# A fused attention kernel: the first unit's maxima move in among the last projections

## The reference

```
q, k, v = x @ Wq.T, x @ Wk.T, x @ Wv.T          # 32 heads of 16
q, k    = rope(q), rope(k)
scores  = q k^T / 4 + bias[head, i - j]          # bias where 0 <= i - j < 256, causal
m       = max(max_j scores, offset[head])
p       = exp(scores - m);  out = (p v) / (sum p + exp(offset - m))
x1      = layernorm(x + out @ Wo.T)
result  = layernorm(x1 + mxfp4(x1) @ mxfp4(Wff).T + bff)
```

## Time and profile before

| | |
|---|---|
| median of 3 runs | 1731.51 us (1725.53 to 1735.53) |
| profiled execution | 1733.33 us |
| its span, first to last instruction | 1731.5 us |
| busy: PE, DVE, ACT, POOL | 86%, 74%, 51%, 15% |
| mean granted TensorE clock | 0.932 of full |

### The profile page before, as it was taken

One profiled execution on the slowest core, in us unless ns is written; L12 is line 12 of the kernel. 1 busy time (PEld: TensorE's weight loads), 2 busy tenths in 40 slices (PEclk: granted clock), 3 DMA queues, 4 the chain that ended last, 5 costly groups with the idle time before them and its releaser, 6 DMA issues.

```text
span 1731.5 us, 60636 instructions
## 1 busy us (share of the span) xinstructions
PE 1497.2 (86%) x22568; PEld 858.3 (50%) x22576; DVE 1286.1 (74%) x3807; ACT 877.9 (51%) x1168; POOL 263.2 (15%) x120
## 2 busy tenths in 40 slices
PE   5978887838999999899999899999899999888773
PEld 4766666612555445455455455455455454443331
DVE  4454545469888788788788788788788883489996
ACT  3333333310665566566566565566566667445442
POOL 4434343440000000000000000000000000044543
PEclk9988898855999999999999999999999999999995
DMA  5444444475363273154245245345344402012221
GB/s 187 144 146 145 146 142 150 127 183 76 76 102 54 60 111 62 53 106 75 52 90 88 56 79 78 67 76 84 72 75 74 83 25 94 25 49 97 73 73 48
DMA packets 127101, 155.94 MB, mean 90 GB/s; under 512 B 18240, under 2 KB 82880, under 8 KB 126560
## 3 DMA queue, kind: packets, MB, share of 16 engines
q1 hardware_dynamic: 126816, 152.12, 38.3%
HBM read 100.78 MB, written 50.50 MB: 87 GB/s over the span
## 4 chain that ended last, share of the span: by engine, by line
PE 44%; DVE 23%; issue 19%; POOL 7%; ACT 3%; DMA 1%; DVEq 1%; SPq 0%; ACTq 0%; POOLq 0%
PE ps L728 10%; PE ps L707 10%; PE ps L687 10%; PE ps L713 6%; DVE junk L1211 6%; DVE mx L1204 4%; POOL probs L1076 4%; PE ps L660 4%; PE ps L820 2%; POOL h_lo L1062 2%; PE ps L738 1%; DVE mx L1211 1%; DVE probs L1178 1%; DVE parts L1155 1%; POOL probs L1116 1%
## 5 line engine op out<-in xcount | busy, mean ns | idle before, releaser
L929 ACT ACTIVATE probs<-ps 128x1024 f32<-128x1024 f32 (+3 forms) x768 | 603.2, 812 | 383.2 <-PE ps L713 332.6
L1211 DVE CUSTOM_DVE_ANT_0 junk<-ps,bias_q 128x384 bf16<-128x384 f32 (+2 forms) x1024 | 500.0, 502 | 123.0 <-PE ps L687 104.2
L687 PE MATMUL ps<-stack 96*32 96x384 bf16 (+3 forms) x6144 | 524.7, 341 | 59.6 <-DVE mx L1211 32.4
L707 PE MATMUL ps<-stack 99*32 99x512 bf16 (+3 forms) x6144 | 519.4, 333 | 11.8 <-issue 9.4
L1204 DVE TENSOR_REDUCE mx<-ps 128x1 f32<-128x128 f32 (+3 forms) x768 | 362.5, 485 | 27.0 <-PE ps L687 22.0
L713 PE MATMUL ps<-toep,flip 96*32 96x384 bf16 (+2 forms) x5120 | 374.9, 284 | 1.9 <-issue 1.8
L728 PE MATMUL ps<-probs,v_sb 128*32 128x512 f32 (+3 forms) x3072 | 322.0, 490 | 0.1
L687 PEld LDWEIGHTS ps<-stack 96*32 96x32 bf16 x6144 | 171.8, 97 | 298.9 <-DVE mx L1211 105.0
L707 PEld LDWEIGHTS ps<-stack 99*32 99x32 bf16 x6144 | 170.8, 96 | 140.4 <-issue 70.9
L1111 POOL TENSOR_TENSOR stack<-stack,bias_q 128x1024 f32<-128x1024 f32 x16 | 37.6, 2347 | 1110.1 <-ACT stack L989 1110.1
L713 PEld LDWEIGHTS ps<-toep,flip 96*32 96x32 bf16 x5120 | 146.9, 99 | 58.8 <-issue 7.5
(11 more groups left out here) (97 smaller groups left out, 1440.9 us busy)
## 6 DMA issues: line engine op xcount, KB each, us to landing
stack<-q_parts SPq DMA_DIRECT2D x192, 128.0 KB, 4.2
stack<-k_parts SPq DMA_DIRECT2D x192, 128.0 KB, 4.2
v_dram<-v_sb SPq DMA_DIRECT2D x32, 512.0 KB, 2.7
v_sb<-v_dram SPq DMA_DIRECT2D x128, 128.0 KB, 4.0
q_parts<-parts SPq DMA_DIRECT2D x96, 128.0 KB, 1.9
k_parts<-parts SPq DMA_DIRECT2D x96, 128.0 KB, 2.0
h_raw<-hT SPq DMA_DIRECT2D x8, 1024.0 KB, 6.2
stack<-h SPq DMA_DIRECT2D x16, 512.0 KB, 3.9
```

Source lines behind the costliest of these rows:

```text
L687: mm = pe.matmul(ps_ring[STRIP * a:STRIP * (a + 1), use.bank, 0:c1 - c0], q_stack[b][0:STACK, hl, i:i + STRIP], k_stack[b][0:STACK, hl, c0 ...
L707: mm = pe.matmul(ps_s[STRIP * a:STRIP * (a + 1), u % 2, hh, 0:w], k_stack[b][0:ROWS, hl, j:j + STRIP], q_stack[b][0:ROWS, hl, i0:i0 + w], ...
L929: act.activation(probs[:, (u // 2) % 3, 2 * pr:2 * pr + 2, 0:w], ps_s[:, pr, :, 0:w], ACT.Exp).then_inc(exp_done, 1)
L1211: ins = dve.tensor_tensor_reduce(out=junk[:, use.bank, 0:c1 - lo], in0=ps_ring[:, use.bank, lo - c0:c1 - c0], in1=bias_q[:, hl, BAND - t0 ...
```

## The change

Three edits go together. ACT takes the next pair's banks up before it splits the present pair, in all batches. The projections use five banks, 3 to 7, so that the ring's three are free. In the last batch PE issues two of unit 0's 48 maxima with each of the 24 projections, one in its middle and one behind it, each as a single matmul of full width (128 columns of weights) in place of four strips; DVE reduces four of them ahead of the first pair and six in each pair, at three places. Unit 0's stack and bias are loaded during the third batch; unit 1's stack during the last pair of the last batch, once all projections are done. POOL splits the extended bias (L1087 to L1093) before phase 1 and not after it, and SP stores it there. The early SBUF tensors are laid out in another order.

```
+PROJ_BANKS = 8 - RING
+EARLY_MAX = 4
+def proj_bank(k):
+    return RING + k % PROJ_BANKS
+def proj_earlier(k):
+    if k >= PROJ_BANKS:
+        return k - PROJ_BANKS
+    return max(j for j in range(24) if j % PROJ_BANKS == k) - 24
...
 SP, phase1
+                        if isinstance(b, int) and b == 2:
+                            first_loads(pair)
                         wait_then_address(v_ready, FIRST + b * 8 + pair + 1)
...
+                        if last and pair == 7:
+                            sp.wait_ge(proj_done, 96)
+                            load_stack(0, 1, 1)
...
 PE
+            def first_maximum(k):
+                I, c0, c1 = MAX_UNITS[k % NMU]
+                hl = k // NMU
...
+                use = Use.first(0, k)
+                wait_use(use)
+                pe.matmul(ps_ring[:, use.bank, 0:c1 - c0], q_stack[0][0:STACK, hl, I * P:(I + 1) * P],
+                          k_stack[0][0:STACK, hl, c0:c1], start=True, stop=True).then_inc(ring_filled, 1)
 PE, phase1, projection k
-                        bank = k % 8
-                        wait_bank(b, k - 8)
+                        bank = proj_bank(k)
+                        wait_bank(b, proj_earlier(k))
...
+                            if last and kt == 1:
+                                first_maximum(2 * k)
                         mm.then_inc(proj_done, 1)
+                        if last:
+                            first_maximum(2 * k + 1)
...
 ACT, phase1
+                take_up(0)
                 for pair in range(8):
-                    take_up(pair)
-                    split(pair)
+                    if pair < 7:
+                        take_up(pair + 1)
+                    split_high(pair)
+                    split_middle(pair)
...
 DVE, phase1
+                if last:
+                    first_maxima(range(EARLY_MAX))
...
                         (by_cos)
+                        if last:
+                            first_maxima(range(EARLY_MAX + 6 * pair, EARLY_MAX + 6 * pair + 2))
...
                         (rot, third_part of the pair before)
+                        if last:
+                            first_maxima(range(EARLY_MAX + 6 * pair + 2, EARLY_MAX + 6 * pair + 4))
                         dve.wait_ge(rot_hi, b * 8 + pair + 1)
                         (rest)
+                        if last:
+                            first_maxima(range(EARLY_MAX + 6 * pair + 4, EARLY_MAX + 6 * pair + 6))
```

More of the change, by code:

```diff
@@ L552, in phase1 @@
                         load_hT(b * 2 + c + 2)
-            loop_and_peel(sp, B, phase1)
+            with sp.Fori(0, B - AHEAD) as b:
+                phase1(b, False)
+            for b in range(B - AHEAD, B):
+                phase1(b, b == B - 1)
             for i in range(4):
@@ new lines, in phase1 @@
+            def phase1(b, last):
+                for c in range(NCH):
+                    pe.wait_ge(h_high, b * 2 + c + 1)
+                    pe.wait_ge(h_low, b * 2 + c + 1)
+                    for i in range(12):
+                        k = c * 12 + i
+                        bank = proj_bank(k)
+                        wait_bank(b, proj_earlier(k))
+                        w = 2 if i % 3 == 2 else i // 6
+                        pe.wait_ge(w_high[w], 2)
+                        pe.wait_ge(w_low[w], 2)
+                        for kt in range(NK):
+                            for j, (wp, hp) in enumerate(((w_hi, h_hi), (w_hi, h_lo), (w_lo, h_hi))):
+                                if w < 2:
+                                    m = i % 3 * 2 + i // 3 % 2
+                                    lhsT = wp[w][:, kt, m * P:(m + 1) * P]
+                                    rhs = hp[c][:, kt, :]
+                                else:
+                                    lhsT = hp[c][:, kt, i // 3 * P:(i // 3 + 1) * P]
+                                    rhs = wp[2][:, kt, :]
+                                mm = pe.matmul(ps[:, bank, :], lhsT, rhs, start=(kt == 0 and j == 0),
+                                               stop=(kt == NK - 1 and j == 2))
+                            if last and kt == 1:
+                                first_maximum(2 * k)
+                        mm.then_inc(proj_done, 1)
+                        if last:
+                            first_maximum(2 * k + 1)
@@ L751, in _ @@
+            with pe.Fori(0, B - 1) as b:
+                phase1(b, False)
+            pe.wait_ge(ident_ready, 7)
+            pe.wait_ge(ones_set, 3)
+            phase1(B - 1, True)
+            transpose_shift(0, Use.first(0, NM))
+            maxima(0, 1, range(NM), lambda k: Use.first(1, k))
+            transpose_shift(1, Use.first(1, NM))
+            pe.wait_ge(raw_ready, FIRST + 32)
+            pe.wait_ge(v_ready, FIRST + 32)
             pe.wait_ge(ones_set, 6)
@@ L1083, in _ @@
             pool.wait_ge(sin_ready, FIRST + 32)
[L1086 to L1094, removed]
             pool.wait_ge(rot_lo, 32)
@@ L1265, in normalise, with first_maxima @@
                                   ALU.mult).then_inc(ring_read, 1)
[L1267 to L1273 removed]
+            def first_maxima(ks):
+                for k in ks:
+                    if k < NM:
+                        max_unit(0, k, 0, Use.first(0, k))
@@ new lines, in _ @@
+            with dve.Fori(0, B - 1) as b:
+                phase1(b, False)
+            dve.wait_ge(off_loaded, 16)
+            dve.tensor_scalar(neg_off[:, :], off[:, :], -1.0, None, ALU.mult).then_inc(neg_off_ready, 1)
+            dve.wait_ge(neg_off_ready, 1)
+            dve.wait_ge(ident_ready, 4)
+            phase1(B - 1, True)
+            shifts(0, 0, 0, Use.first(0, NM - 1))
+            split_shifts(0, Use.first(0, NM))
+            for k in range(NM):
+                max_unit(0, k, 1, Use.first(1, k))
@@ L1275, in _ @@
+            shifts(0, 1, 1, Use.first(1, NM - 1))
+            dve.wait_ge(shift_loaded[0], 16 * PARTS)
+            split_shifts(1, Use.first(1, NM))
+            dve.wait_ge(v_ready, FIRST + 32)
+            dve.wait_ge(ext_stored, 16)
+            dve.wait_ge(sin_ready, FIRST + 32)
             MASK = 0x7F800000
```

147 lines of the change are left out of this document (58 added, 89 removed).

## The result

The changed kernel takes **1765.38 us** (median of 4 runs, 1765.09 to 1770.00), the one before 1730.94 in the same rounds (4 runs, 1725.53 to 1735.53): ratio 1.0203, 95% interval 1.0175 to 1.0230. It is slower by 34 us; 1734 was forecast. The profiled execution took 1770.0, 4.6 more than the median, and its span is 1768.2.

A forecast was written before the change was run, and what follows sets the result against it. A chain across DVE, POOL and ACT paces projections; DVE paces maxima. Terms -22 + 31 - 24.3 + 12 = -3 us, plus 5 margin, gave +2 to +3 against 1731.5: 1734 us, range 1717 to 1750.

The forecast's parts named there:

- The look-ahead: First three batches: taking up the next pair early removes the wait for `raw`; third batch ends at 264, -22 us.
- my bounds of -12 and -30: First three batches: -12 if DVE and POOL collide more often, -30 if the chain at chunk changes hides behind PE.
- the chain through the change of chunk: Nine projections, then ACT, DVE and POOL steps in series: 36.5 us, 38.5 with margin, per chunk instead of 43.1.
- POOL's ext split: Moved ahead of phase 1, it was to cost the first pair about 5 us.
- The last batch: Projections with unit 0's maxima among them: 121 us instead of 90.2, +31, with DVE ending phase 1 at 385.
- The ring wait: Last batch: PE stands 3.9 us behind each pair's v projection until DVE reads a tile; a pair takes 13.3 us.
- some of the nine 3.9 us gaps may be answered with the half rate (2): Last batch: a 2 us margin for PE's clock falling after some of the waits behind v projections.
- rival 2: Last batch: half rate after every gap, or DVE and POOL colliding in each pair; 1744 to 1757, taken as 1746; chance 0.30.
- The hole: Before unit 1's first tile: DVE idles about 12 us because stack 1 is issued late behind pair 6's stores.
- Unit 1's maxima: Stage before phase 2: as long as today, 25.2 us from unit 1's first tile to phase 2.
- Phase 2 unchanged: Phase 2 and all behind it: the change touches nothing there, so it stays at 1303.5 us.
- the stages behind it: After the last batch: unit 0's stage goes, -24.3 us net, and the wait for stack 1 adds 12.

The follow-up runs named there:

- look_only: The kernel before, with only ACT's look-ahead added (eight banks, no early maxima, old loads): 1721.52 us, ratio 0.9932.
- h_later: The changed kernel, with the next input's h load issued behind the next chunk's first store of v, not ahead of it: 1754.26 us, ratio 1.0119.
- v_behind: The changed kernel, with only q and k taken up ahead and the next pair's v behind the present pair's split: 1720.19 us, ratio 0.9913.
- v_behind8: The kernel before (eight banks, late maxima, old loads), with q and k taken up ahead and v behind the split: 1687.32 us, ratio 0.9745.
- no_look: The changed kernel with ACT's old order, taking up a pair and then splitting it: 1737.86 us, ratio 1.0024.
- stack_early: The changed kernel, with unit 1's stack issued ahead of pair 6's stores of parts: 1757.52 us, ratio 1.0135.
- both_pad: The changed kernel with v taken up behind the split, stack 1 issued early, and 288 unused semaphore increments starting PE's program: 1728.85 us, ratio 0.9979.
- loads_wide: The kernel before with q, k ahead, v behind the split, unit 0's loads in the third batch, first two units' maxima full-width: 1680.52 us, ratio 0.9701.
- loads_5banks: The kernel before with q, k ahead, v behind the split, unit 0's loads in the third batch, five banks: 1675.37 us, ratio 0.9672.

## Why the prediction was wrong

**The look-ahead, -22 us: wrong, and the step that failed.** It said that ACT takes up v (0.6) on its way to the high part. That priced the take-up and not the wait in front of it. v's buffer is free when the store of two pairs before has landed, and moving the take-up ahead of the split moved it ahead of that. Measured -2, with 46.0 us of waits, outside my bounds of -12 and -30; look_only has the same waits without the rest of the change, and h_later turns 13.6 us less of them into 13.7 us. With v alone put back (v_behind) it is -33, beyond my bound of -30: the chain through the change of chunk seems to hide behind PE, which was busy for 212.76 of the first 252.60 us. The prediction had a row that showed this wait, 9.30 us in the earlier trace rows, and read it as an effect of unit 0's loads alone. For that one place v_behind8 bears it out; but the prediction didn't ask which old wait a moved instruction meets earlier, and so never looked for it in the other batches.

**POOL's ext split, 5 us: about 3.5.** The first `rest` came at 38.9 for 32.6, but most of that isn't the split: look_only, where the split stands behind phase 1 as before, has its first `rest` at 37.5. no_look has the split and no look-ahead, and 36.1.

**The last batch, 121 us: the mechanism right, the size off.** The ring wait was there behind the v projections at 3.44 to 3.57 us where 3.9 was forecast, and no_look, in which `rest` doesn't stand behind the next v, has no such gaps. The change of chunk took 23.8 us from `rest` to `rest`, where 23.7 was forecast. What was mis-sized is the term "some of the nine 3.9 us gaps may be answered with the half rate (2)": the other five intervals are 14.3 to 15.7 us, 15.0 on average, for 13.3, which makes 8 of the 10 us. PE was busy 87.05 us for 309 matmuls; at 0.2245 each, the price of the earlier trace rows, they are at most 69.4, so half rate cost 17.7 us or more. Some 4 of them were in the forecast, at the start of the batch and at the change of chunk. That is rival 2, right in its clock, its place and its price: it added 9 to 23 us, took 12 for its 1746, and had a chance of 0.30. Its 1746 stayed below the measured time because the look-ahead's -22 is in it too; its 12 us and the look-ahead's 20 make 1766, which is in part luck, since phase 2's 8 us aren't in that sum. The Trainium skill (TensorE: Matmul & The Clock Gate, "Why this matters for your kernels") warns of such gaps between bursts, and the trace agrees: the clock fell behind each of the gaps of 3.4 to 3.6 us. The runs go further: in v_behind it fell behind three of four gaps of 2.04 to 2.09 us too.

**The hole, 12 us: right.** DVE stood 14.6 us, PE 15.3; last issue to landing 11 us, as in the earlier trace rows. The reason was right too: stack_early took 13.5 us of it away.

**Unit 1's maxima:** 24.9, as forecast.

**Phase 2 unchanged: 8 us off, cause not settled.** Up to 4.6 of these may be this one execution, which lay that much above the median. All six kernels with early maxima and without padding show 1055.6 to 1062.1 us, and those without early maxima 1042.1 to 1051.9, so there is something. In the profiles 6.8 of the 8 us stand in the units at the two jumps back, as the place of the code in PE's program would have it; the medians of both_pad and loads_wide bear out 1 and 2 us only. The new layout of the early SBUF tensors, the order of the loads ahead of phase 2, and the state in which the queues enter it weren't tried apart.

**The sum:** 20 (look-ahead) + 10 (last batch) - 3 (the stages behind it, whose margins were not used up) + 8 (phase 2) = 35 above the forecast; 34.2 is the profiled span's difference to 1734. The range reached to 1750 for rival 2. With the look-ahead at its measured -2 the forecast would have been 1754.

**What the edits are worth,** read from the table: look-ahead for q and k alone and the loads moved, -54.7 us (1733.0 in the same rounds to 1678.27); v ahead of the split, -45 when undone; stack 1's place, -8 to -18 when mended (13.5 and 13.6 at the first score matmul); early maxima with both of these mended, +26.5 against loads_5banks (1701.86 and 1675.37), which has the same five banks; in this are the SBUF layout and the ext split, which weren't tried alone. Each figure carries some 3 to 5 us of noise. The last one is 41 us more in the last batch (109.2 for 68.2), less the some 22 that come back until phase 2 starts (at the first score matmul the difference is 19.8); 10 more stand in phase 2 in the profiles (1057.5 for 1047.6), 7.4 of them in the units at the jumps.

## What to carry to other kernels

An instruction moved ahead in its engine's program meets every one of its waits earlier; list them all, that for its output buffer's store too, and ask where in the DMA queue that store stands. Work put between the matmuls of a bound engine may use idle time only if that time is still there when the other edits are in, and if no step of the chain it feeds is queued behind that engine's newest result; otherwise each round pays the wait and the clock's return to 2.4 GHz. Split a change like this one: here the good part of it was worth 55 us and was hidden under three that cost 90 together (45 for v's place, 18 for stack 1's, 27 for the early maxima).

## What the hardware showed

- The granted clock was 0.50 behind each of the gaps of 3.4 to 3.6 us that had matmuls after them; behind the one at 361.39 it fell 0.4 us later, behind the others at once; behind the one at 345.84, 14 matmuls ran at 0.41 us each before it came back. In v_behind it fell within 1.4 us of the end of three gaps of 2.04 to 2.09 us (274.78, 330.22, 343.26), for 3.3 us each, and stayed at 1.00 behind a fourth (318.51).
- A store of v waited 8.6 us from issue to use (251.48 to 260.10) behind a load that had been issued 1.5 us earlier; in h_later, with the load behind it, it was 4.3 us (240.78 to 245.03).
